# First two layer norms of a four-layer gated kernel: variance on all partitions by one product with ones, root on ScalarE, reciprocal on VectorE

## The reference

```
def _layernorm(x, axis=-1, eps=1e-05):
    m = jnp.mean(x, axis=axis, keepdims=True)
    v = jnp.var(x, axis=axis, keepdims=True)
    return (x - m) / jnp.sqrt(v + eps)
...
x = x + jnp.tanh(g_xattn[0]) * _L0_xattn_ref(_layernorm(x, axis=-1), ctx_1024, ctx_1024)
x = x + jnp.tanh(g_ffn[0]) * _L0_ffn_ref(_layernorm(x, axis=-1), L0_ffn_gate_w, ...)
x = x + jnp.tanh(g_xattn[1]) * _L1_xattn_ref(_layernorm(x, axis=-1), ctx_1024, L1_xattn_wq, ...)
```

## Time and profile before

| | |
|---|---|
| median of 3 executions | 588.36 us (587.42 to 590.1) |
| the profiled execution | 593.04 us, of which the span of its records is 591.3 us |
| busy in the span | PE 561.5, DVE 441.2, ACT 402.5, POOL 102.0 us |
| granted clock of TensorE, mean | 0.988 of full speed |

### The profile page before, as it was taken

How to read it: one execution, slowest core, us unless ns; L and a number is a source line. 1 busy time by engine, 2 the same in 40 slices (tenths; PEclk the granted TensorE clock), 3 DMA queues, 4 the chain that set the end, 5 groups by cost and what they waited for, 6 DMA issues and landing times.

```text
span 591.3 us, 8732 instructions
## 1 busy us (share of the span) xinstructions
PE 561.5 (95%) x3258; PEld 388.0 (66%) x3258; DVE 441.2 (75%) x692; ACT 402.5 (68%) x561; POOL 102.0 (17%) x69
## 2 busy tenths in 40 slices
PE   8999999898999999999896999999999999999997
PEld 5688887656777867764330346566546767888886
DVE  3477988768749799986889676676768938787786
ACT  3799899765856755426999774624514858888875
POOL 5400000001110000004989703200000310000000
PEclk8999999999999999999899899999999999999999
DMA  6118020300100459110000024505610110812100
GB/s 241 39 36 321 37 71 1 116 1 2 55 1 2 162 209 262 48 52 1 7 1 1 1 72 103 184 3 163 158 35 2 38 38 2 314 46 70 35 2 35
DMA packets 19342, 43.81 MB, mean 74 GB/s; under 512 B 2090, under 2 KB 7594, under 8 KB 19300
## 3 DMA queue, kind: packets, MB, share of 16 engines
q1 hardware_dynamic: 19300, 43.25, 23.1%
HBM read 42.55 MB, written 0.70 MB: 73 GB/s over the span
## 4 chain that ended last, share of the span: by engine, by line
PE 72%; DVE 15%; ACT 8%; issue 3%; POOL 1%; DVEq 0%; ACTq 0%; POOLq 0%
PE ps L818 35%; ACT work L1217 5%; PE ps L860 4%; PE ps L800 3%; PE ps L569 3%; PE ps L552 3%; DVE h_lo L1754 2%; PE ps L844 2%; PE ps L846 2%; PE ps L885 2%; PE ps L845 2%; PE ps L685 2%; PE ps L559 2%; PE ps L658 2%; DVE h_act L1727 2%
## 5 line engine op out<-in xcount | busy, mean ns | idle before, releaser
L1754 DVE TENSOR_TENSOR h_lo<-h_act,h_hi 128x512 fp32r<-128x512 f32 (+1 forms) x114 | 103.7, 914 | 39.8 <-ACT h_hi L1264 39.0
L818 PE MATMUL ps<-n_hi,w_hi 128*128 128x512 f32 x224 | 86.6, 421 | 2.4 <-DVE h_act L1727 1.2
L1264 ACT CAST h_hi<-h_act 128x1024 fp32r<-128x1024 f32 (+1 forms) x88 | 75.4, 856 | 14.6 <-PE ps L818 11.9
L818 PE MATMUL ps<-n_hi,w_lo 128*128 128x512 f32 x224 | 79.7, 391 | 0.0
L818 PE MATMUL ps<-n_lo,w_hi 128*128 128x512 f32 x224 | 79.5, 390 | 0.0
L1967 POOL TENSOR_TENSOR rstd<-var_eps,minus_half 128x4 f32<-128x4 f32 x16 | 17.1, 1070 | 312.8 <-DVE var_eps L1409 312.8
L1217 ACT ACTIVATE work<-work,p_rest 128x2048 f32<-128x2048 f32 x31 | 59.4, 1994 | 0.4 <-DVE work L1607 0.4
L1257 ACT ACTIVATE h_act<-ps 128x512 f32<-128x512 f32 x44 | 26.3, 598 | 45.6 <-PE ps L818 45.3
L818 PE MATMUL ps<-h_hi,w_hi 128*128 128x512 f32 x162 | 56.3, 396 | 0.1
L1994 POOL TENSOR_TENSOR work<-xc,txt 128x2048 f32<-128x2048 f32 x15 | 54.0, 3624 | 9.2 <-ACT xc L1181 7.9
L818 PE MATMUL ps<-h_hi,w_lo 128*128 128x512 f32 x162 | 55.4, 390 | 0.0
(11 more groups left out here) (235 smaller groups left out, 1043.2 us busy)
## 6 DMA issues: line engine op xcount, KB each, us to landing
work<-g_rows SPq DMA_DIRECT2D x36, 512.0 KB, 5.8
w_f<-in_w SPq DMA_DIRECT2D x20, 512.0 KB, 3.6
w_f<-in_w SPq DMA_DIRECT2D x8, 384.0 KB, 3.3
work<-g_rows SPq DMA_DIRECT2D x8, 256.0 KB, 7.0
work<-g_rows SPq DMA_DIRECT2D x4, 384.0 KB, 6.7
diag<-in_w SPq DMA_DIRECT2D x2, 512.0 KB, 5.1
work<-in_w SPq DMA_DIRECT2D x2, 512.0 KB, 4.5
w_f<-in_w_rest SPq DMA_DIRECT2D x2, 384.0 KB, 4.1
```

What stands on the lines that cost most here:

```text
L818: mm = pe.matmul(dst[i], wap(wt, e, lo, size, rows), mv[i], start=(first and c == 0), stop=(last and c == 2))
L1264: act.copy(places(h_hi, m, step), places(h_act, m, step)).then_inc(s["hi"], 1)
L1754: dve.tensor_tensor(lo, src, hi.bitcast(F32), ALU.subtract).then_inc(s["lo"], 1)
```

## The change

For the norms in `ROOTED = (0, 1)` and both halves:

- `norm_var` becomes one product: weights are a 128x128 matrix of ones, the moving operand `sq` with 512 columns. Every partition receives the sum over the features of every token.
- `norm_root` (new, ACT): in place in PSUM, square root of (sum / 128 + eps).
- `norm_out`: in place in PSUM a reciprocal of 128x512 on VectorE, then the product with `xc`.
- `norm_eps`, `norm_power` and `norm_spread` do nothing for these norms.
- ScalarE's order: a load of the Sqrt table after the tanh of the gates, a load of the Gelu table after the fourth root; the split of expert 0's down weights and that of expert 1's up weights move behind that load, and `norm_high(1, 0)` stands ahead of the third `copy_keys` and of the root of (1, 1).

```
             def norm_var(j, t):
                 pe.wait_ge(ln["sq"], 2 * j + t + 1)
+                if j in ROOTED:
+                    pe.matmul(ps[:, LNBANK[j, t][1]], ones_w[:, :], sq[:, half(t)], start=True, stop=True).then_inc(ln["var"], 1)
+                    return
...
+            def norm_root(j, t):
+
+                act.wait_ge(ln["var"], 2 * j + t + 1)
+                var = ps[:, LNBANK[j, t][1]]
+                act.activation(var, var, ACT.Sqrt, bias=eps_w[:, 0:1], scale=1.0 / P).then_inc(ln["std"], 1)
...
             def norm_out(j, t):
-                dve.wait_ge(ln["bc"], 2 * j + t + 1)
                 dve.wait_ge(ln["xc"], 2 * j + t + 1)
+                if j in ROOTED:
+                    dve.wait_ge(ln["std"], nth_root(j, t))
+                    root = ps[:, LNBANK[j, t][1]]
+                    link(dve.reciprocal(root, root))
+                    dve.tensor_tensor(n[:, half(t)], xc[:, half(t)], root, ALU.mult).then_inc(ln["n"], 1)
+                    return
+                dve.wait_ge(ln["bc"], nth_power(j, t))
...
@@ scalar stream
             act.activation(tg, tg, ACT.Tanh).then_inc(tg_ready, 1)
+            load_table(ACT.Sqrt)
             for t in range(2):
                 norm_square(0, t)
             act.wait_ge(in_ctx, 16)
             for t in range(2):
                 act.activation(diag[:, half(t)], ctxT[:, half(t)], ACT.Square).then_inc(pre["kv"], 1)
+                norm_root(0, t)
                 norm_copy(0, t)
...
             copy_keys(0, 0, 0)
-            split_hi_down(MOES[0], 0)
+            norm_root(1, 0)
             copy_keys(0, 0, 1)
             norm_square(1, 1)
             norm_copy(1, 1)
-            split_hi_up(MOES[0], 1)
             norm_high(1, 0)
             copy_keys(0, 1, 0)
+            norm_root(1, 1)
+            act.activation(table[:, 4:5], ones_w[:, 0:1], ACT.Gelu)
+            split_hi_down(MOES[0], 0)
+            split_hi_up(MOES[0], 1)
             copy_keys(0, 1, 1)
             split_hi_down(MOES[0], 1)
...
@@ vector stream
             dve.memset(ones_w[:, :], 1.0)
+            dve.memset(eps_w[:, :], EPS)
```

More of the change, by code:

```diff
@@ L142 @@
 ]
+ROOTED = (0, 1,)
 PACKS = {
@@ L215, in flamingo @@
         ones_w = sb("ones_w", [P, P])
+        eps_w = sb("eps_w", [P, 1])
         starts = {e: sb(f"starts{e}", [P, TILES * e]) for e in (8, 16)}
@@ L259, in flamingo @@
         g_half = work[:, 4 * T:12 * T].rearrange("p (e t) -> p e t", e=16)
-        table = sb("table", [P, 1])
+        table = sb("table", [P, 8])
         plain_second, plain_rest = diag, kT[1][:, 0:MOES[1].rest * MOES[1].sizes[-1]]
@@ L293, in flamingo @@
         x_done = [sem("x_done0"), sem("x_done1")]
-        ln = {k: sem(f"ln_{k}") for k in ("mean", "xc", "sq", "var", "eps", "rstd", "bc", "n", "hi", "lo")}
+        ln = {k: sem(f"ln_{k}") for k in ("mean", "xc", "sq", "var", "std", "eps", "rstd", "bc", "n", "hi", "lo")}
         pre = {k: sem(f"pre_{k}") for k in ("kv", "scan", "proj", "k", "v", "vcp", "kcp", "txt", "txtcp", "uv", "uvcp", "uv_dram", "uv_in", "wo")}
@@ L400, in query_part, with nth_power, nth_root @@
             return 0 if p < HT else p // 2 - 1
+        def nth_power(j, t):
+            return 2 * (j - len([o for o in ROOTED if o < j])) + t + 1
+        def nth_root(j, t):
+            return 2 * ROOTED.index(j) + t + 1
         def halves_of(t):
@@ L562, in norm_spread @@
             def norm_spread(j, t):
-                pe.wait_ge(ln["rstd"], 2 * j + t + 1)
+                if j in ROOTED:
+                    return
+                pe.wait_ge(ln["rstd"], nth_power(j, t))
                 if LNBANK[j, t][2] == LNBANK[j, t][0]:
@@ L1054, in load_table @@
             def load_table(function):
-                act.activation(table[:, :], minus_half[:, 0:1], function)
+                at_col = (ACT.Exp, ACT.Gelu, ACT.Silu, ACT.Sqrt).index(function)
+                act.activation(table[:, at_col:at_col + 1], ones_w[:, 0:1], function)
             def copy_values(i, q):
@@ L1964, in norm_power @@
             def norm_power(j, t):
+                if j in ROOTED:
+                    return
                 r = slice(t * HT, (t + 1) * HT)
-                pool.wait_ge(ln["eps"], 2 * j + t + 1)
+                pool.wait_ge(ln["eps"], nth_power(j, t))
                 pool.tensor_tensor(rstd[:, r], var_eps[:, r], minus_half[:, r], ALU.pow).then_inc(ln["rstd"], 1)
```

5 lines of the change are left out of this document (3 added, 2 removed).

## The result

The change made the kernel slower by about twice what was forecast: 598.75 us, median of 6 executions (597.08 to 599.43), against 589.73 of the kernel before (6 executions, 587.42 to 591.57). The medians stand 9.0 us apart; the recorded ratio is 1.0139, with a 95% interval of 1.0112 to 1.0166, that is +8.2 us (6.6 to 9.8), and the text goes by that. The forecast was +4.3, and 592.7 with a range that ended at 596.0.

A forecast was written before the change was run, and what follows sets the result against it. TensorE, 72% of the chain, was taken to bound the kernel. A 4.3 us delay on the path plus 0.06 for the `eps_w` fill gave +4.3, or 592.7 us against the 588.36 median; range 590.0 to 596.0.

The forecast's parts named there:

- The price of the reciprocal: VectorE, norms 0 and 1: a straight line from small sizes gives 3.35 us per 128x512 reciprocal, four making 13.4 us.
- Norm 0 and norm 1, half 0: Start of the kernel: x of norm 0 done at 16.1 and 23.0 us, `n` of norm 1 at 27.1, 5.0 late.
- ScalarE's queue and TensorE: Norm 1 into the experts: queue delays the fourth key copy to 32.3 us, so TensorE's values product is 4.3 us late.
- that rival: ScalarE table switches: drain counts too, a switch holding ScalarE 2.8 us, not 1.42; +6.6, 595.0 us; 3 in 100.
- The other branch: Norm 1's fourth reciprocal, `n`, rounding and low part: ready near 35.0 us, product due at 35.6, so 0.6 early, no bound.
- the paragraph on GpSimd: Expert 0's low parts on GpSimd: no longer behind powers; down part there at 32.3 us, needed at 36.
- Behind it: All after the start: TensorE keeps its 4.3 us delay, ScalarE wins back 1.2 us, no wait for an absolute time.
- The sentence on loads: Later transfers: loads are issued when a buffer is freed, so they move with the rest.
- The cold-TensorE rival: TensorE's new idle gaps before 33 us drop its clock: 594.3 to 596, say 594.6 us; 18 in 100.
- the two stretches at 0.53 and 0.62: TensorE at 10 to 14 us in the kernel before: granted clock at the lower level, 1.2 GHz, for most of them.
- Its sentence that a fall before 23 us costs nothing: Cold-TensorE rival, start of the kernel: a clock fall before 23 us costs nothing, since VectorE sets the time.
- The 1.2 us that I gave those stretches: Norm 0's spread before the change: 16 matmuls took 3.53 us against 1.16 for 8 at 2.4 GHz, 1.2 us lost.

The follow-up runs named there:

- no_recip: The changed kernel with the four reciprocals of norms 0 and 1 left out, n computed as xc times the root: 590.14 us, ratio 1.0008 to the kernel before.

## Why the prediction was wrong

The direction was right, and so were the sizes at the start, but for one meeting of VectorE and GpSimd; the total was half of what was measured.

**The price of the reciprocal** was right: 3.35 forecast from sizes of 4 to 64, 3.36 measured.

**Norm 0 and norm 1, half 0.** Forecast 16.1 and 23.0 us for x, 27.1 for `n`; the trace has 15.4, 22.3 and 26.3. All is 0.7 to 0.8 sooner because the first mean came sooner in this execution (its square began at 6.30 us, at 7.16 before). That is no gain of the change's: in its two other traces the square came at 7.46. The steps between are as worked out: from the first square to the first expert product the three traces take 2.7 to 2.9 us more than before, and 2.75 had been forecast.

**ScalarE's queue and TensorE.** The fourth key copy ended at 31.2 (32.3 forecast, 0.8 of it that same shift), TensorE waited 1.13 us (1.6). The table load held the queue 1.4 us, from 28.08 to the cast at 29.48. The 2.66 us of the Trainium skill (ScalarE: Activation LUTs, "What ACT_TABLE_LOAD costs") did not appear, here as in the earlier trace rows, and that rival is out.

**The other branch** I called 0.6 us early; it was 0.4 late. The step behind that is the paragraph on GpSimd, which asked only when its results are needed. The split of expert 0's down weights had moved behind the root on ScalarE, so GpSimd's low parts ran from 30.16 to 33.91 us and met VectorE there: `h_lo` took 1.50 us and not 0.69. Before, GpSimd was done when that instruction began. It cost about 0.4 us of the path, which is what the start is late beyond the 4.3, counted from the first square.

**Behind it** is the step that failed: "Whatever delay it has when the experts run evenly, it keeps", so that the sum has a term of nothing for all that follows the start. The clock with which TensorE runs the rest was taken to be that of before, and for that no reason was given. The kernel before, in three traces, passes everything between 15 and 290 us at full clock. The change loses 1.5 to 2.7 us between 115 and 150 us in all three of its traces, where the clock falls once or twice. In sum, by traces: 4.4 at the start, 2.3 there, 0.3 to 319 us, nothing in the mean behind it, 7.0. All executions give 8.2 (6.6 to 9.8). Two of the three traces of before are long executions, with 14.5 us at the lower clock against 7.2 in the mean, which makes the 7.0 a low count.

The sentence on loads, "they move with the rest", holds for the change, but not for a lead: in `no_recip` the spread gates came 0.9 us after VectorE was ready for them.

The cold-TensorE rival, at 18 in 100, had the right mechanism in the wrong place: I looked for it in the gaps that the change opens and priced it there at up to 3 us. Filled gaps gave 1.2, within the noise. Its sentence that a fall before 23 us costs nothing was right: the change's traces with 3.4 and 6.8 us at the lower clock there reach the experts equally late from the first square. I read the two stretches at 0.53 and 0.62 as belonging to one place, and did not ask what the clock does behind the start. The 1.2 us that I gave those stretches in the kernel before is 0.9 by the trace of the pure delay.

What stays open is why the clock falls at these two places in more executions of the change. A delay alone of 4.3 us brought hardly more time at the lower clock (8.3 us against 7.9), one of 2.1 us brought 5.3 us more. Both kernels stay under the change's 17.3 us, of which 3.4 to 6.8 lie at the start, where they cost nothing. So how much of the excess belongs to the delay and how much to the change's own activity isn't shown. With one trace a kernel I can say that unchanged code was passed at full clock or at 0.88, not how often each happens.

## What to carry to other kernels

A reciprocal is priced by the column: on values that are the same for all partitions, compute it where they are narrow and spread the result, not the other way round. One or two microseconds can depend on whether TensorE's clock falls in code that the change doesn't touch; so compare a change also against the same kernel with a plain delay at its start, in many executions, before giving its loss or gain to its parts. And two profiles of one kernel differed by 3.6 us here, nearly half the effect: lay three side by side at common instructions, counted from the same first step, before reading a difference.

## What was not expected of the hardware

- The same instructions ran at a granted clock of 1.00, 0.94 or 0.88 over 29 us, and how late the program was doesn't tell which: 1.00 and 0.94 at 3.4 us late, 0.88 at 4.4 and 1.00 at 4.5. In every trace the falls between 40 and 285 us came at the same two places of the program.
- A delay of 2.1 us cost 4.5 in the mean, the delay alone in six executions and 5 us more in five; one of 2.0 more on top of the change cost nothing that can be measured.
- VectorE's subtraction of two 128x512 operands in SBUF took 1.50 us, and 1.75 in another order, instead of 0.69 while GpSimd ran a subtraction of its own; the scan of `no_recip` took 2.29 instead of 1.22 in the same way. The Trainium skill (SBUF — State Buffer, "SBUF: two separate sides") describes a pair of ports that either engine takes for a whole instruction while the other waits. The trace agrees: `h_lo` began at 32.97, while GpSimd's third subtraction ran to 33.91, and ended at 34.47, 0.56 us after it. The reciprocal, at 3.36 us from PSUM, was not stretched by GpSimd's work beside it.
